# Reciprocal deviations ahead of evictions, the last softmax shift and the second values one slot sooner: a transformer layer on eight cores

## The reference

```
def _layernorm(x, axis=-1, eps=1e-5):
    m = jnp.mean(x, axis=axis, keepdims=True)
    v = jnp.var(x, axis=axis, keepdims=True)
    return (x - m) / jnp.sqrt(v + eps)

q = (src @ Wq + bq).reshape(B, nb, bs, H, dk)      # bs = 64, H = 8, dk = 128
k = (src @ Wk + bk).reshape(B, nb, bs, H, dk)
v = (src @ Wv + bv).reshape(B, nb, bs, H, dk)
scores = jnp.einsum('bnqhd,bnkhd->bhnqk', q, k) * dk ** (-0.5)
probs = jax.nn.softmax(scores, axis=-1)
out = jnp.einsum('bhnqk,bnkhd->bnqhd', probs, v).reshape(B, S, D)
return out @ Wo + bo

h = jnp.square(jax.nn.relu(jnp.einsum('bsd,fd->bsf', x, W_fc)))
y = jnp.einsum('bsf,df->bsd', h, W_proj)
# five steps of a leaky counter over y; its output is spikes / 5

x = x + attention(layernorm(x))
x = x + ffn(layernorm(x))
```

## Time and profile before

| | us |
|---|---|
| median of 3 runs | 712.77 (712.08 to 713.43) |
| profiled execution, its own time | 712.98 |
| its span, slowest core (core 3) | 711.4 |
| spans of the eight cores | 708.4 to 711.4 |
| TensorE busy | 695.0 (98%) |
| DVE busy | 383.6 (54%) |
| ACT busy | 171.4 (24%) |
| mean granted TensorE clock, by core | 0.998 to 0.999 |

### The profile page before, as it was taken

How to read it: one execution, slowest core, us unless ns; L and a number is a source line. 1 busy time by engine, 2 the same in 40 slices (tenths; PEclk the granted TensorE clock), 3 DMA queues, 4 the chain that set the end, 5 groups by cost and what they waited for, 6 DMA issues and landing times.

```text
span 711.4 us, 10652 instructions; the slowest of 8 cores (708.4 to 711.4 us)
## 1 busy us (share of the span) xinstructions
PE 695.0 (98%) x3804; PEld 325.3 (46%) x3804; DVE 383.6 (54%) x573; ACT 171.4 (24%) x314; POOL 50.2 (7%) x96
## 2 busy tenths in 40 slices
PE   8899999999999999999999999999999999999996
PEld 4444444444444444444444444444444444444444
DVE  5325775676587466427846226855225766221476
ACT  3453330441252035030003331002332001332000
POOL 2111110121004200000000000000000000000000
PEclk9999999999999999999999999999999999999999
DMA  8997986598649994598262002162002051100011
GB/s 182 200 163 142 165 149 187 119 220 202 142 131 221 227 241 73 147 174 209 77 196 84 0 1 60 52 188 104 12 1 61 30 147 65 53 1 1 30 44 45
DMA packets 31010, 80.92 MB, mean 114 GB/s; under 512 B 5616, under 2 KB 5872, under 8 KB 30192
## 3 DMA queue, kind: packets, MB, share of 16 engines
q0 software_dynamic: 12960, 31.46, 26.0%
q1 hardware_dynamic: 15552, 40.39, 19.7%
q10 hardware_dynamic: 2448, 8.40, 3.1%
HBM read 82.33 MB, written 16.78 MB: 139 GB/s over the span
## 4 chain that ended last, share of the span: by engine, by line
PE 91%; DMA 4%; DVE 3%; issue 1%; ACT 1%; POOL 0%; DVEq 0%; ACTq 0%; POOLq 0%
PE ps_m L415 31%; PE ps_y L487 30%; PE ps_m L362 11%; PE ps_m L388 8%; PE ps_m L402 8%; DMA wq_sb<-Wq 4%; DVE acc_sb L733 1%; PE ps_y L441 1%; PE ps_y L469 1%; PE ps_m L494 1%; PE ps_t L453 0%; DVE blk L673 0%; DVE acc_sb L730 0%; DVE e_sb L681 0%; DVE ssum L688 0%
## 5 line engine op out<-in xcount | busy, mean ns | idle before, releaser
L415 PE MATMUL ps_m<-xn2t,w_sb 128*128 128x512 bf16 x1024 | 223.0, 379 | 0.1
L487 PE MATMUL ps_y<-w_sb,h_sb 128*128 128x512 bf16 (+1 forms) x1024 | 218.3, 376 | 0.0
L415 PEld LDWEIGHTS ps_m<-xn2t,w_sb 128*128 128x128 bf16 x1024 | 99.7, 98 | 119.3
L487 PEld LDWEIGHTS ps_y<-w_sb,h_sb 128*128 128x128 bf16 x1024 | 100.2, 98 | 117.6
L573 ACT ACTIVATE h_sb<-ps_m 128x512 bf16<-128x512 f32 x128 | 76.5, 598 | 266.6 <-PE ps_m L415 266.4
L723 DVE TENSOR_TENSOR h_sb<-h_sb 128x512 bf16<-128x512 bf16 x128 | 53.2, 424 | 125.9 <-ACT h_sb L573 125.9
L733 DVE SCALAR_TENSOR_TENSOR acc_sb<-ps_y,acc_sb 128x1024 bf16<-128x1024 f32 (+2 forms) x72 | 78.6, 1092 | 7.9 <-DVE acc_sb L730 0.5
L362 PE MATMUL ps_m<-xnt,wq_sb 128*128 128x512 bf16 x240 | 56.7, 379 | 2.9 <-DMA wq_sb<-Wq 2.9
L362 PE MATMUL ps_m<-xnt,wk_sb 128*128 128x512 bf16 x248 | 58.6, 379 | 0.5 <-DMA wk_sb<-Wk 0.5
L388 PE MATMUL ps_m<-wv_sb,xnt 128*128 128x512 bf16 x256 | 56.9, 379 | 0.0
L402 PE MATMUL ps_m<-wo_sb,attn_sb 128*128 128x512 bf16 x256 | 55.9, 379 | 0.4 <-ACT attn_sb L591 0.4
(11 more groups left out here) (63 smaller groups left out, 344.4 us busy)
## 6 DMA issues: line engine op xcount, KB each, us to landing
xr<-x SPq DMA_DIRECT2D x32, 512.0 KB, 6.6
xl<-x SPq DMA_DIRECT2D x96, 128.0 KB, 4.3
w_sb<-Wfc POOLq DMA_DIRECT2D x32, 256.0 KB, 8.8
x<-xr ACTq DMA_DIRECT2D x16, 512.0 KB, 5.2
out<-xr POOLq DMA_DIRECT2D x12, 512.0 KB, 3.1
w_sb<-Wpr POOLq DMA_DIRECT2D x16, 256.0 KB, 32.5
xn2t<-blk SPq DMA_DIRECT2D x64, 64.0 KB, 2.0
w_sb<-Wpr POOLq DMA_DIRECT2D x4, 1024.0 KB, 15.1
```

The costliest lines, as they stand in the source:

```text
L415: m = E.matmul(bank(key)[:], w1_sb[fc // 4][:, k0:k0 + 128], tokens(xn2t, c, 0, 4), start=(c == 0), stop=(c == 7))
L487: return E.matmul(out, h_sb[fc][:, tt * 128:(tt + 1) * 128], w2_sb[fc // 4][:, k0:k0 + n], start=(fc == 0), stop=(fc == 31))
```

## The change

Three edits in the table of slots and in ACT's list. No instruction is added or removed; 1403, 518, 311, 65 and 102 instructions or runs of like ones stand on TensorE, DVE, ACT, GpSimd and SyncE before and after. GpSimd's and SyncE's lists are unchanged.

```
 def softmax_pair(b, s):
-    return s // 4 if b >= 0 and s % 4 == 0 and s < 16 else None
+    slots = [0, 4, 8, 12 if b == 0 else 11]
+    return slots.index(s) if b >= 0 and s in slots else None
...
 def values_four(b, s):
-    slots = [16, 24] if b == 0 else [13, 19]
+    slots = [16, 24] if b == 0 else [13, 18]
     return slots.index(s) if b >= 0 and s in slots else None
...
# scalar_program
                 if (f := values_four(b, s)) is not None:
                     value_copy(b, 4 * f)
                     value_copy(b, 4 * f + 1)
-                if b == -1 and (i := ln_unit(b, s, LN_RSTD)) is not None:
+                if (i := ln_unit(b, s, LN_RSTD)) is not None:
                     ln_rstd(i)
                 if key[0] != "v":
                     main(key)
...
                 if (j := softmax_pair(b, s)) is not None:
                     exps(b, j)
-                if b >= 0 and (i := ln_unit(b, s, LN_RSTD)) is not None:
-                    ln_rstd(i)
```

## The result

The changed kernel takes 709.14 us (median of 6 runs, 708.27 to 710.89), the kernel before in the same session 713.10 us (6 runs, 712.08 to 713.52). The ratio is 0.995 with a 95% interval of 0.9938 to 0.9962, so 2.7 to 4.4 us were won; 709.2 had been forecast. The profiled execution took 710.89 us, its slowest core (core 7) spans 709.2 us. Fifteen executions of the later sessions (nine of the kernel before, six of variants) took 746.6 to 852.9 us, with mean granted clocks from 0.81 to 0.98 on the four cores of one die, and are left out of every time and ratio here.

The account below looks back on a forecast made before the run. TensorE, busy 98% of the 711.4 us span, was the bound; 3.13 us (values, blocks 1 and 2) plus 0.55 (block 3) made 3.68 at most, 3.6 taken: median 712.77 becomes 709.2 us, range 708.4 to 710.6.

Parts of the forecast that it names:

- The bound and the cause: TensorE bounds; its values wait 3.0 us in total for the last softmax shift, block 3's output group 0.4 for a copy.
- Part 1: Reciprocal deviations ahead of the eviction on the scalar engine: vector engine 1.2 us sooner, the 1.50 us wait cut to about 0.3.
- Part 2: Last softmax shift one slot sooner in blocks 1 to 3: ends 1.1 us before the values are due, so their wait goes.
- The slack in the ring: Blocks 1 and 2: slot 12's eviction ends about 149.1, its bank is wanted at slot 15 at 151.77; 2.6 us left.
- Part 3: Second values at slot 18 in place of 19: nothing won in blocks 1 and 2, 0.38 to 0.55 us in block 3.
- the margin: Slot 18 in block 1: last transposed pair's copy ends 158.08, slot 17's group 158.75, so 0.67 us are left.
- the rival of a new wait at slot 18: Vector engine late to slot 17 by 1.24 us overdraws 0.67 by 0.57 in blocks 1 and 2: 710.3 us; chance 6%.
- The sum: Gains in blocks 1 to 3 together: 3.37 us at least, 3.68 at most, 3.6 taken.
- The half that stays: Statistics wait for late rows in blocks 1 and 2, so some 1.5 of 3.1 us stay: 710.8 us; chance 6%.
- The chances: Whole kernel, by more than 0.2% (1.4 us): faster 0.94, within 0.03, slower 0.03.
- the first two rivals: A new wait at slot 18 (710.3 us, chance 6%) and half of the values' wait staying (710.8 us, chance 6%).
- The rule on the clock: Skill's limiter takes a die with three dense cores to 13/16 clock: 37 us more in blocks 1 to 3; trace disagrees.

Follow-up runs that it names:

- consumer-later run: Kernel before with, in blocks 1 to 3, the first values at slot 14 not 13 and the third pair's transposes at 15 not 14; ratio to before 0.9954.
- filler run: Changed kernel with four idle matmuls ahead of the wait for the fifth head's Wq in block -1; 709.15 us, ratio to the kernel before 0.9942.

## Why the prediction held

**The bound and the cause** were right. Behind the start, TensorE's only waits were those of the earlier trace rows on line 469 and on the output group, and both are gone. The consumer-later run shows the cause in another way.

**Part 1.** The scaling was to lose its wait and the sum to come 1.2 us sooner. On the scale of before the sum starts at 143.64 - 1.70 = 141.94 (141.9 forecast, 143.14 before). Alone the part was to leave about 0.3 us of wait; it left 0.28.

**Part 2.** Shift from 146.49 - 1.70 = 144.79 (144.8 forecast) to 146.23 (146.3); values at 147.51 (147.51 forecast); the eviction of slot 12 at 148.33 (148.4), and slot 15 at 151.77 (151.77). With the shift alone TensorE was to wait 0.1 and waited 0.08. The slack in the ring held as well: the eviction ends at 149.00, so 2.77 us are left for 2.6 forecast, and with the deviations another slot sooner nothing reached TensorE, with two 0.99 us did.

**Part 3.** 0.55 us forecast for block 3, 0.5 measured (40.81 to 40.29); by itself 0.4. The 1.73 us a group are the distance from start to start; the row that was given for it, 13.97 us for eight groups, makes 1.75, and 0.52 in place of 0.55. The term that was mis-sized is the margin. "0.67 us are left" was worked out from the end of the copy to the end of slot 17's group, as if the values could start at the copy's end; the hand-over was put at nothing. They start 0.47 behind it, and the margin is 0.29 in blocks 1 and 2. The 0.15 us of the earlier trace rows would have been too little as well, since there the late wait stands last of four. So the rival of a new wait at slot 18 was more than twice as near as it was priced.

**The sum.** 3.6 us forecast; the blocks gave 3.8, the medians 4.0 with 2.7 to 4.4 as the interval of the ratio. Block 1 gave 1.57 on cores 1 and 3 and 1.67 on the others, block 2 1.75 on these two cores and 1.56 on the others. The excess has two sources that the sum didn't have. In block 1, on the six cores with 1.67, the 32 matmuls of the values themselves took 0.11 us longer behind their wait (0.68 us to the next group for 0.57); without a wait they take 0.57 on every core, so this is part of what the change wins. In block 2, on cores 1 and 3, the scores were shown at 0.94 and 0.83 us, and at 0.79 both in the changed kernel. That is not a gain of the three parts: the filler run, with the change in place, has 0.92 on six cores and 59.27 to 59.38 in block 2. What makes either group of small matmuls longer on one core or in one kernel than in another stays open.

**The half that stays** named a real thing: the statistics of slot 15 wait 1.72 us for their rows on core 7, because they are now taken sooner. They are over before the cast starts at 157.20, and the copy that the second values need follows at 157.81, so nothing stays of the old waits. But the wait eats the idle time that spoke against a late vector engine at slot 17: 0.29 us are left ahead of the cast, where over 1 us had been counted on. The prediction priced the late rows and the new wait at slot 18 as two rivals; the traces show them as one chain, late rows, late copy, late values. It cost 0.05 us on one of the 16 cores in the two profiles of the changed kernel, and rows that land later still would cost more. That it stayed so small is in part luck, since the chain's slack was not worked out.

**The chances.** The forecast and the first two rivals add up to 0.95, not 0.94.

**The rule on the clock.** The granted clock is 1.00 in blocks 1 to 3 of the changed kernel's cores too, with no idle time left, so denser work did not lower it in any profile here, and the 37 us that the prediction worked out came in no execution that the times count. Where it did fall in the profiles, it was behind an idle stretch and not in a busy one. The Trainium skill, page "TensorE: Matmul & The Clock Gate", part 1, says that the gate goes by how busy TensorE has been and samples it with a free-running window, so that the same program comes out differently from run to run. The traces agree that it comes out differently: 3 of 16 cases fell after 1.81 us of idling, none of 16 after 1.50 in the kernel before, and in the start of one execution core 4 fell after 2.03 and core 5 didn't after 2.23. The sampling itself no run here can show.

## What to carry to other kernels

When one engine writes for another in a table of slots, read the last writer's end and the first reader's due time on one scale: here they told the wait and its cure to a tenth of a microsecond, and moving the producer one slot sooner or the consumer one slot later was worth the same. Add the hand-over to every margin too, and take it from a row in which as many waits stand behind the late one. Two edits that bring the same event forward don't add up; the second buys margin, and whether that is worth its place is a question of what else it could hold up. Of several waits ahead of one instruction, put the one that comes last at the end of the row.

## What the runs showed of the hardware

- On TensorE three met waits that stand behind the late one cost 0.31 us after the release. With three behind it the first weight load came 0.44 us after the copy's end, with none 0.12 after the shift's; moving the wait took 0.3 off each idle time, or put 0.3 on.
- An idle time of 1.81 us ahead of 32 small matmuls dropped the granted clock to the 1.2 GHz level in 3 of 16 cases and cost 1.7 us each time, nearly as much as the wait itself. At 1.50 us it never did in the 16 cases of the kernel before. A wait a little longer than another can so cost double. Yet 2.52 us in the start of the consumer-later run left the clock at 1.00 while 2.03 us in another run lowered it, so the length of one idle time doesn't tell whether a fall follows.
- The 32 small matmuls right behind a wait took 0.68 us in place of 0.57 in block 1 of the kernel before on six of eight cores, and 0.57 to 0.58 in block 2 behind the same wait. Why, no run here shows.
